# Four mixed layers on one core: nine merges of the work by cost shares become one merge by a written table of turns

## The reference, cut to what matters

```python
xn = _layernorm(x, axis=-1)
s = attention(xn)          # layers 0, 1, 3 causal; layer 2 with binary weights, not causal
g = _silu(branch(xn))
x = x + s * g
```

```python
def step(carry, _):
    u, v = carry
    u = -jax.nn.logsumexp(Z + v[..., None, :], axis=-1)
    v = -jax.nn.logsumexp(Z + u[..., :, None], axis=-2)
    return ((u, v), None)
(u, v), _ = jax.lax.scan(step, (u0, v0), None, length=num_iters)   # num_iters = 50
```

## Time and profile before

| | us |
|---|---|
| median of 3 runs (1438.63 to 1447.93) | 1445.67 |
| the profiled execution | 1444.44 |
| span of that execution | 1442.7 |
| TensorE busy over the span | 1098.7 (76%) |
| VectorE busy | 871.4 (60%) |
| ScalarE busy | 578.9 (40%) |
| GpSimd busy | 320.4 (22%) |
| mean granted TensorE clock | 0.871 |

### The profile page before, as it was taken

The page is one execution under the profiler, slowest core; times in us unless marked ns, Lnnn a source line. Parts: engine busy times, 40 slices in busy tenths (PEclk is TensorE's granted clock), DMA queues, the critical chain, the costliest instruction groups (busy, mean ns, idle before and its releaser), DMA issues.

```text
span 1442.7 us, 20140 instructions
## 1 busy us (share of the span) xinstructions
PE 1098.7 (76%) x7480; PEld 446.7 (31%) x7480; DVE 871.4 (60%) x1777; ACT 578.9 (40%) x801; POOL 320.4 (22%) x514
## 2 busy tenths in 40 slices
PE   2889998977788568648437367878788988898887
PEld 1434443433233223314213012312222233333333
DVE  4222221005667589885898887657667587736663
ACT  2433332003554423145114146574445555434452
POOL 1145542017722101011011053700100031111220
PEclk9889999996999678768678588988789999999999
DMA  7322210012100002001101021401012111211100
GB/s 278 118 66 66 69 62 0 0 45 85 46 21 18 7 18 66 12 1 51 33 17 52 24 68 43 131 17 39 17 32 63 51 42 31 70 47 30 52 17 30
DMA packets 54901, 69.74 MB, mean 48 GB/s; under 512 B 9526, under 2 KB 43444, under 8 KB 54800
## 3 DMA queue, kind: packets, MB, share of 16 engines
q1 hardware_dynamic: 50828, 58.58, 12.9%
q0 software_dynamic: 3984, 9.98, 2.3%
HBM read 49.45 MB, written 18.82 MB: 47 GB/s over the span
## 4 chain that ended last, share of the span: by engine, by line
PE 36%; DVE 31%; ACT 5%; issue 4%; SPq 1%; DMA 1%; ACTq 0%; DVEq 0%
DVE w_mx L1404 13%; PE w_banks L669 10%; PE w_po L1319 9%; PE w_banks L1301 4%; PE w_banks L1273 4%; DVE w_region L1891 3%; PE w_banks L1261 2%; ACT w_pr L1347 2%; DVE w_region L1888 2%; DVE w_region L1869 2%; DVE w_region L1886 2%; PE w_banks L1329 2%; PE w_banks L1555 2%; DVE w_region L1884 1%; DVE w_region L1882 1%
## 5 line engine op out<-in xcount | busy, mean ns | idle before, releaser
L1404 DVE TENSOR_REDUCE w_mx<-w_banks 128x2 f32<-128x1024 f32 (+3 forms) x352 | 376.8, 1086 | 195.7 <-PE w_banks L1273 191.4
L1347 ACT ACTIVATE w_pr<-w_banks 128x1024 f32<-128x1024 f32 (+1 forms) x312 | 315.0, 1013 | 429.6 <-PE w_banks L1301 428.3
L1386 POOL TENSOR_SCALAR_AFFINE_SELECT w_pr<-w_pr 128x512 f32<-128x512 f32 (+1 forms) x184 | 104.6, 569 | 561.1 <-ACT w_pr L1347 561.0
L1301 PE MATMUL w_banks<-w_qs,w_ks 49*128 49x512 f16 (+7 forms) x832 | 136.7, 353 | 89.9 <-DVE w_mx L1404 58.8
L1273 PE MATMUL w_banks<-w_ks,w_qs 48*128 48x512 f16 (+7 forms) x832 | 145.0, 361 | 40.5 <-DVE w_mx L1404 23.3
L1319 PE MATMUL w_po<-w_pr,w_vz 128*17 128x512 f32 (+7 forms) x1152 | 154.2, 561 | 12.7 <-ACT w_ou L1369 12.7
L78 PE MATMUL f_pp<-xt,sl_region 128*128 128x512 f16 x672 | 148.9, 382 | 3.5 <-POOL sl_region L508 3.5
L1261 PE MATMUL w_banks<-mask_half,ident_half 64*128 64x128 bf16 (+1 forms) x768 | 67.3, 255 | 37.8 <-DMA w_ks<-stack_scratch 17.1
L482 DVE TENSOR_TENSOR sl_region<-sl_region,f_pp 128x512 f32<-128x512 f32 x28 | 19.2, 687 | 121.1 <-ACT sl_region L497 121.1
L78 PEld LDWEIGHTS f_pp<-xt,sl_region 128*128 128x128 f16 x672 | 65.1, 98 | 84.6 <-issue 5.3
L1301 PEld LDWEIGHTS w_banks<-w_qs,w_ks 49*128 49x128 f16 (+1 forms) x832 | 41.7, 98 | 138.5 <-issue 57.5
(11 more groups left out here) (222 smaller groups left out, 1513.9 us busy)
## 6 DMA issues: line engine op xcount, KB each, us to landing
stack_scratch<-sl_region SPq DMA_DIRECT2D x102, 128.0 KB
w_qs<-stack_scratch SPq DMA_DIRECT2D x96, 96.0 KB, 2.4
sl_region<-in_L_gu SPq DMA_DIRECT2D x14, 512.0 KB
w_stage<-in_L_w POOLq DMA_DIRECT2D x36, 128.0 KB, 2.4
sl_region<-in_L_down SPq DMA_DIRECT2D x14, 256.0 KB
stack_scratch<-p_qk SPq DMA_DIRECT2D x24, 128.0 KB
w_ks<-stack_scratch SPq DMA_DIRECT2D x32, 96.0 KB, 2.6
bw_stage<-in_L_w SPq DMA_DIRECT2D x4, 640.0 KB, 11.8
```

The costliest lines, as they stand in the source:

```text
L1301: mm = pe.matmul(g.banks.pair_at(f)[:, half, at:at + T - q0], g.ks[base:base + self.rows + 1, k_slot, k_place, j * P:(j + 1) * P], g.qs[ba ...
L1347: act.activation(g.probs.at(self.pr_fill[s])[:, :, 0:width], g.banks.pair_at(self.s_fill[s])[:, :, 0:width], ACT.Exp, scale=self.a.scale). ...
L1386: pool.affine_select(out=diagonal, in_=diagonal, compare_op=ALU.is_ge, fill=0.0, base=0, pattern=pattern, channel_multiplier=-1).then_inc( ...
L1404: dve.tensor_reduce(out, g.banks.pair_at(self.m_fill[m])[:, :, 0:heads * keys].rearrange("q h (p k) -> q h p k", k=keys), AX.X, ALU.max).t ...
```

## The change

Five edits. First, x comes in four transfers of two row tiles each in place of one, each with a semaphore, and the statistics of the norm wait for them pair by pair. Second, in the same stage ScalarE makes the high halves of the weights ahead of those of x, and GpSimd makes all four low halves, where it shared them with VectorE. Third, in the feed-forward branch the first two slabs read their down scale where it lies (`sv_d`), so two small transfers (line 445) go, and GpSimd makes the low half of gate and up (line 508) ahead of that of down (line 506), with a semaphore count after each. Fourth, all attentions now load their row of ones at tick -4; only the first one did it at its first tick. Fifth, the nine merges become one, in which a table says which strand comes next and for how many ticks. The strand `a` holds all attention bodies, `b` all outputs, norms, projections and leads, `s` the streams, `r` the routed branches, `w` the weights, `l` the small transfers, `c` the lead of `a01`. No instruction of the woven part is added or taken away.

```diff
@@ norm_and_split
-            if x_in is not None:
-                sp.dma_start(g.x_res[:, :, :], x_in).then_inc(x_here, 16)
+            for k, here in enumerate(x_here):
+                sp.dma_start(g.x_res[:, 2 * k:2 * k + 2, :], x_in[:, 2 * k:2 * k + 2, :]).then_inc(here, 16)
...
             for t in range(NT):
+                if t % 2 == 0:
+                    dve.wait_ge(x_here[t // 2], 16)
                 dve.bn_stats(st[:, t, :], g.x_res[:, t, :]).then_inc(stats, 1)
...
-            for k, (_, staged, h, l) in enumerate(splits):
-                if k % 2 == 0:
-                    dve.wait_ge(w_hi, k + 1)
-                    dve.tensor_tensor(l, staged, h, ALU.subtract).then_inc(w_lo, 1)
...
             for k, (_, staged, h, l) in enumerate(splits):
-                if k % 2:
-                    pool.wait_ge(w_hi, k + 1)
-                    pool.tensor_tensor(l, staged, h, ALU.subtract).then_inc(w_lo, 1)
+                pool.wait_ge(w_hi, k + 1)
+                pool.tensor_tensor(l, staged, h, ALU.subtract).then_inc(w_lo, 1)
@@ swiglu_low_rank
-                    wait_pos(sp, lo, i - 1)
+                    wait_pos(sp, lo, i * 2 - 2)
                     if not isinstance(i, int) or i > 1:
                         load_slab(sp, ins, ws, i, u, w_here[u])
-                    sp.dma_start(svd[:, u, :], sv_d[:, ds(i * P, P)]).then_inc(w_here[u], 16)
+                        sp.dma_start(svd[:, u, :], sv_d[:, ds(i * P, P)]).then_inc(w_here[u], 16)
...
+                    pool.tensor_tensor(wgu[:, u, 1, :], ws[:, u, 0:gu], wgu[:, u, 0, :], ALU.subtract).then_inc(lo, 1)
                     pool.tensor_tensor(wd[:, 1, ds(i, 1), :], ws[:, u:u + 1, gu:gu + down], wd[:, 0, ds(i, 1), :],
-                                       ALU.subtract)
-                    pool.tensor_tensor(wgu[:, u, 1, :], ws[:, u, 0:gu], wgu[:, u, 0, :], ALU.subtract).then_inc(lo, 1)
+                                       ALU.subtract).then_inc(lo, 1)
@@ Attend
-        self.ones_tick = self.first if before is None else -4
+        self.ones_tick = -4
@@ merge, weave
+TURNS = """
+    a2 w2 a2 w6 l w2 a2 w a14 w a w a3 w a2 w a2 w2 a w a10 w a2 w2 a w a2 c2 a c3 w a c a3 w c2 a3 c a c a c a c w2
...
+def merge(strands, turns, order, emitted, banks):
...
+    for turn in turns.split():
+        letter, count = turn[0], int(turn[1:] or 1)
+        for stage, t in flat[letter][at[letter]:at[letter] + count]:
...
+            stage.plan(t)
+            order.append((stage, t))
```

More of the change, by code:

```diff
@@ L1939, in body_of @@
     return stage, range(0, stage.ticks[-1] + 1)
-def some_of(stage, first, last):
-    return stage, range(first, last)
 class Shared:
@@ L2118, in weave @@
                        + split_rows("L1_wo", wo1, 2) + split_rows("L1_w24", w24) + [(ins["L1_wb"], wb[:, 0], wb[:, 1])])
-        merge([[all_of(small), all_of(a00)], [all_of(split1), lead_of(a01)]], order, emitted, g.banks)
         o00 = Outward(g, h[0], 0, lambda part, c: wo[:, part, c, :], o_rows[:, 0, :], att(0), sl[:, 0], done(a00), None,
@@ L2161, in weave @@
                        [(p11.made, len(p11.chunks)), (p11.v_made, p11.v_units), s1.ready(), (o01.made, NI)])
-        merge([[body_of(a20)], [all_of(o11), all_of(n21), all_of(p21), all_of(r20), lead_of(a21)], [all_of(split3)]],
-              order, emitted, g.banks)
         rows3 = Loads(g, "third", [(g.cos, ins["cos"]), (g.sin, ins["sin"]),
@@ L2177, in weave @@
         split_base = Split(g, split_rows("L3_w_base", w_base), [(o11.gated, NI)])
-        merge([[body_of(a21)], [all_of(rows3), all_of(o20), all_of(n30), all_of(p30), lead_of(a30)], [all_of(r21)],
-               [all_of(split_base)]], order, emitted, g.banks)
         o21 = Outward(g, h[2], 1, lambda part, c: sign_o[:, c, :], g.binary.rows[:, h[2].n_v:], att(1), sl[:, 0], done(a21),
```

105 lines of the change are left out of this document (54 added, 51 removed).

## The result

The changed kernel takes **1323.7 us** (median of 4 runs, 1321.0 to 1331.2) against 1445.4 for the kernel before in the same job: ratio 0.917, 95% interval 0.913 to 0.922. Timed twice more it gave 0.922 (0.919 to 0.925) and 0.920 (0.917 to 0.923). The forecast was 1400, the range ended at 1364: the direction was right, the gain of 120 us is almost three times the 45 that I had summed. The profiled execution took 1323.3 us, span 1321.3, mean clock 0.909.

What follows compares the result with a forecast made beforehand. The woven part was taken as bound by VectorE first, then a mixed stretch, TensorE last. Gains of 6.9 + 2.3 + 1.1 + 5 + 4 + 21 + 5 = 45.3 us gave 1400 us, range 1364 to 1431.

Steps and rivals of the forecast that it cites:

- Step 6: Late stretches: no general gain, as the same strands run in nearly the same relation; last output stage moved, 5 us.
- Rival (c): The late stretches gain as well, 31 of their 62 open us: 1369 us; chance 0.15.
- Step 4: Earlier Sinkhorn: ten maxima move from ahead of sample 0's first step to behind it; 4 us gain, between 0 and 8.
- step 3: Start of the woven part: stacks are issued ahead of small transfers and ones; 5 us gain, between 3.8 and 6.6.
- Step 5: Sample 1's streams under `a20`: 136 Sinkhorn steps between its maxima fill VectorE's idle; 21 us gain, the largest term.
- rival (a): The chain from the last stream instruction to `a21` keeps its length, 147 us: 1471 us; chance 0.05.
- Step 1: The norm: piecewise landing of x and redistributed halves end the stage at 24.7 instead of 31.6; 6.9 us gain.
- rival (d): In the norm, the port lock of VectorE and GpSimd costs 4 us: 1404 us; chance 0.08.
- Step 2: Feed-forward start: 2.3 us from the scale read in place, 1.1 us from swapping lines 508 and 506.
- Rival (b): The merge moves work but gives nothing: 1430 us; chance 0.18; sign: `a20` clock 0.75 with VectorE under 80%.

Runs made afterwards that it cites:

- mended: The changed kernel, but GpSimd's low halves in the norm wait for the normalisation, and small transfers follow the second group's stacks and the ones: 1328.3 us, ratio 0.919.
- order_before: The changed kernel with all its edits except the table's order; the strands stand in the order of the kernel before: 1436.1 us, ratio 0.995.
- mended2: The changed kernel with GpSimd waiting for the normalisation and the small transfers behind the third group's stacks too: 1318.8 us, ratio 0.912; again 1319.3 us, 0.913.
- after: The changed kernel as it is, with all five edits, against the kernel before: 1323.7 us, ratio 0.917.

## Why the prediction was wrong

The forecast was 1400 us and the kernel took 1324, below the range. The ratios of the single parts, against the same kernel before, add up: 0.5% for the front edits, 2.0 for the head, 1.7 to 2.3 for the overlap, 3.4 for the late order, 7.6 to 8.2 in all, and the change has 8.0 (mean of three).

**Step 6, the late stretches: 5 us predicted, 49 measured.** This is the step that failed. Its reason was "the same strands run there in nearly the same relation". That is true of which stages lie beside which, and wrong for where the heavy ticks of a stage lie: 38 of the 49 us stay when only the chains have their old place, and in the two stretches of the last layer the gain goes with the late products of `r30` and `r31` (ticks 33 to 48). What made the 8.8 us in the stretch of `a21` stays open. The table's last lines could have told where those ticks lie, and the earlier trace rows had 62 open us. Rival (c) named the gain at 31 us with 0.15, and as a case for itself, though it excludes none of the other steps. Its point for it, that no engine led in the last stretch, was the better reading of the profile.

**Step 4, the head: 4 us predicted, about 20 to 25 measured** (24 to 29 less the 4 us of step 3, which lie in the same pieces of the table). I priced ten maxima that change sides and did not see the other change in that stretch: `o00` and `n10` end at unit 9, and the burst of 76 stream ticks is gone. Which of the two counts was not taken apart. The first balancing step came 33 us sooner against the start of the woven part, where I had 15. The earlier trace rows showed the room, 30 idle us of VectorE in 423 to 508; now 12 are left in the stretch that answers to it.

**Step 5, the overlap: 21 us predicted, 24 alone, 33 in the table.** The mechanism was right. The chain behind the streams took 908.3 - 843.5 = 65 us, near the 76 assumed, so rival (a) fell. VectorE in 465 to 844 is covered to 90%, as forecast for that stretch.

**Step 1, the norm: 6.9 us predicted, 4.3 measured** (first product of the projection 31.95 to 27.68). The piecewise landing gave its 3.6. But the normalisations took 7.33 us against 3.74, so rival (d) was right in its mechanism: four VectorE instructions were held up, one by each GpSimd half, by 0.9 us each. Of its 4 us 2.6 went from the sum, and with GpSimd kept away the first product comes 3.1 us earlier (`mended`). I had argued from the rule of the Trainium skill, "SBUF — State Buffer", section "SBUF: two separate sides", that the lock concerns VectorE instructions in a 2-port mode or with two SBUF inputs, and I took the normalisation, which has a single tensor input, to be in no such mode without looking at a row. The rows speak for a faster mode: in the kernel before it takes 536 to 545 ns and the next one starts 457 ns after it, while the two-input subtraction `xt<-n_pt,xt` of the same 512 elements takes 679 to 692 ns. No row names the mode. If it is the 2-port one, the trace agrees with the rule, and what was wrong in this step is my premise.

**Step 2: 3.4 us predicted, about 4.5 measured.** The first product of line 78 came 79.42 - 70.63 = 8.8 us earlier, of which 4.3 are step 1; where the last 1.1 came from is open.

**Step 3: 5 us predicted, 4.2 measured** (first exponential 12.1 us earlier, start of the stage 7.9). The first value product is at 335.7, 27.6 us after the stage's start instead of 31.8. TensorE started 7.3 us sooner and then stood 4.6 us for the second group's stacks, which I had called "needed later". `order_before` shows that these 4.2 us are the table's: with the old order, where the small transfers stay ahead of the stacks, the first exponential is 24.2 us behind the first issue, as before. So none of the 12 us was lost on the way, as the expectation for `mended` had it; the old order never had the last 4.

Rival (b), that the merge gives nothing at a low clock, is refuted by the time, and its sign did not come: the clock in 465 to 844 is 0.82, above the 0.74 of the earlier trace rows, with VectorE covered to 90%.

## What to carry to other kernels

When a change replaces the rule that orders the work, cost it by where the longest runs of ticks of one kind lie and which engine they feed, not by which stages overlap. Here a side strand's matmuls cost most among the units of an attention, where ScalarE and VectorE wait for TensorE, and least behind its last unit, where TensorE has holes: 6.6 us of its time made the tail only 3.0 us longer. When several stretches each have idle time, their gains add: make the sum of their mean gains, instead of one forecast with "no gain" and a rival for each.

## What the runs showed of the hardware

- The granted clock changed with nothing but the order: with the same matmuls it was 0.89 in the stretch of `a21` with the old order and 0.98 with the table's. Whether the clock adds to the gain or only shows it was not separated.
- Six runs of one and the same kernel lay between 1321.9 us at a mean clock of 0.911 and 1334.1 at 0.897. This scatter of 0.9% is larger than what the front edits bring; they were better read from the traces.
- A VectorE operation on one SBUF tensor of 128x512 with two scalars per partition takes 541 to 546 ns undisturbed (`mended2`). Beside GpSimd's four subtractions (1.26 to 1.40 us each, 1.21 to 1.22 undisturbed) four of eight took 1.43 to 1.44 us, and each of these ended 0.28 to 0.29 us after one of the subtractions had ended (`after`).
